# Attention and feed-forward layer on one core: the two lengths of score bursts trade units, and blocks of other matmuls go ahead of the fourth score

## The reference

```python
Q, K, V = x @ Wq.T + bq, x @ Wk.T + bk, x @ Wv.T + bv     # x: 2 x 1024 x 512; 32 query, 8 key heads of 16
Q, K = rope(Q), rope(K)                                    # one key head serves 4 query heads
w = softmax(Q K^T / 4)
x = layernorm(x + (w V) @ Wo.T + bo)
g, u = x @ gate_w.T * gate_s, x @ up_w.T * up_s            # 1408 inner columns
x = layernorm(x + (silu(g) * u) @ down_w.T * down_s)
```

## Time and profile before

| what | value |
|---|---|
| median of 3 runs | 1063.87 us (1063.75 to 1064.66) |
| the profiled execution | 1064.13 us, span 1062.3 us |
| PE busy | 1026.5 us, 97% |
| DVE busy | 809.5 us, 76% |
| ACT busy | 665.1 us, 63% |
| POOL busy | 266.2 us, 25% |
| weighings u = 0 to 255 in the trace | from 66.83 us to 796.57 us |
| TensorE clock granted | 0.998 of full speed |

### The profile page before, as it was taken

One profiled execution on the slowest core, in us unless ns is written; L12 is line 12 of the kernel. 1 busy time (PEld: TensorE's weight loads), 2 busy tenths in 40 slices (PEclk: granted clock), 3 DMA queues, 4 the chain that ended last, 5 costly groups with the idle time before them and its releaser, 6 DMA issues.

```text
span 1062.3 us, 15699 instructions
## 1 busy us (share of the span) xinstructions
PE 1026.5 (97%) x5858; PEld 536.8 (51%) x5858; DVE 809.5 (76%) x1199; ACT 665.1 (63%) x1346; POOL 266.2 (25%) x227
## 2 busy tenths in 40 slices
PE   8999999999999999999999999999999999999996
PEld 3643344433443433443444443333337888888885
DVE  4899978899779799779988899999803475662535
ACT  2368877788778788778766678888863431222221
POOL 2751030141335422246200042844100000000002
PEclk9999999999999999999999999999999999999999
DMA  5274417243142512344140446531217510402011
GB/s 200 80 196 126 106 35 213 52 97 78 52 115 75 105 56 54 82 108 105 34 78 12 116 120 150 124 121 37 93 68 193 166 40 9 111 28 52 1 39 42
DMA packets 64432, 94.87 MB, mean 89 GB/s; under 512 B 37536, under 2 KB 37920, under 8 KB 62272
## 3 DMA queue, kind: packets, MB, share of 16 engines
q1 hardware_dynamic: 63776, 93.10, 33.2%
q10 hardware_dynamic: 576, 0.72, 0.2%
HBM read 53.95 MB, written 27.00 MB: 76 GB/s over the span
## 4 chain that ended last, share of the span: by engine, by line
PE 80%; DVE 10%; ACT 6%; issue 2%; DMA 1%; SPq 0%; POOL 0%; DVEq 0%; POOLq 0%
PE PS L448 21%; PE PV L467 20%; PE PSA L537 15%; PE PS L554 5%; PE PSA L426 5%; DVE nmx L964 5%; PE PS L365 4%; ACT Bn L756 3%; PE PS L493 2%; PE PSA L493 2%; DVE nmx L960 2%; DVE nmx L957 2%; ACT Bn L765 2%; PE PV L554 2%; PE PSA L365 1%
## 5 line engine op out<-in xcount | busy, mean ns | idle before, releaser
L756 ACT ACTIVATE Bn<-PS 128x512 f32<-128x512 f32 x1146 | 548.8, 559 | 125.0 <-PE PS L448 111.1
L448 PE MATMUL PS<-Qt,Kt 50*128 50x512 f32 x1146 | 391.7, 434 | 20.0 <-ACT Bn L756 18.7
L426 PE MATMUL PSA<-Kt,Qt 48*128 48x512 f32 x1024 | 390.0, 459 | 2.2 <-DVE Kt L936 0.8
L964 DVE TENSOR_REDUCE nmx<-PSA 128x1 f32<-128x1024 f32 x256 | 312.2, 1219 | 61.0 <-PE PSA L426 59.8
L448 PEld LDWEIGHTS PS<-Qt,Kt 50*128 50x128 f32 x1146 | 184.4, 184 | 323.6 <-ACT Bn L756 312.7
L467 PE MATMUL PV<-Bn 128*32 128x512 f32 x2048 | 272.8, 605 | 0.0
L426 PEld LDWEIGHTS PSA<-Kt,Qt 48*128 48x128 f32 x1024 | 174.6, 183 | 21.7 <-DVE nmx L964 6.2
L960 DVE TENSOR_REDUCE nmx<-PSA 128x1 f32<-128x512 f32 x256 | 174.5, 682 | 1.4 <-PE PSA L426 1.1
L957 DVE TENSOR_REDUCE nmx<-PSA 128x1 f32<-128x512 f32 x256 | 174.3, 681 | 0.0
L537 PE MATMUL PSA<-x1Th,wr 128*128 128x512 f32 x344 | 135.0, 393 | 0.8 <-DVE sg L1052 0.5
L537 PE MATMUL PSA<-x1Tl,wr 128*128 128x512 f32 x344 | 134.7, 392 | 0.0
(11 more groups left out here) (166 smaller groups left out, 919.4 us busy)
## 6 DMA issues: line engine op xcount, KB each, us to landing
Qt<-pscr SPq DMA_DIRECT2D x90, 128.0 KB, 4.9
A<-in_wf SPq DMA_DIRECT2D x11, 768.0 KB, 6.3
wr<-A SPq DMA_DIRECT2D x33, 256.0 KB, 2.9
pscr<-A SPq DMA_DIRECT2D x16, 512.0 KB, 3.7
vscr<-Bn SPq DMA_DIRECT2D x32, 256.0 KB, 2.0
Kt<-pscr SPq DMA_DIRECT2D x90, 64.0 KB, 2.3
A<-A SPq DMA_DIRECT2D x16, 256.0 KB, 3.7
Bn<-vscr SPq DMA_DIRECT2D x8, 512.0 KB
```

Source lines behind the costliest of these rows:

```text
L426: op = e.matmul(PSA[:, 2 * s + h, :], Qt[n % 3][p:p + NC_, g % 2, 128 * qt:128 * qt + 128], Kt[n % 3][p:p + NC_, 512 * h:512 * h + 512], s ...
L448: e.matmul(PS2[:, i, cols], Kt[n % 3][rows, 128 * kt:128 * kt + 128], Qt[n % 3][rows, g % 2, 512 * qh + cols.start:512 * qh + cols.stop], ...
L756: e.activation(Pb[c % NP_][:, cols], PS2[:, score_bank[c, p], cols], ACT.Exp, scale=0.25).then_inc(*act_exp.next(piece(c, p)))
L964: e.tensor_reduce(nmx[:, hh % 2, c0:c0 + 1], slot_pair(s), AX.XY, ALU.max, negate=True).then_inc(*dve_max[s].next(k))
```

## The change

The bursts trade places. `weigh(u - 1)` now stands behind the third score of odd units and behind the fourth of even ones, and the cut score is the fourth of odd units (`c % 8 == 7`). The block of an odd unit goes directly behind that weighing, ahead of the unit's fourth score (`background`), and uses the banks that are free there (`free_banks`). ACT moves a projection out ahead of the fourth exponential. DVE takes only the first half of the unit's second step ahead of its work for the block, and the second half, with the closing of the round, behind it. The closing is cut into three functions with the same four operations.

PE at the first block of the loop, before: the last matmul of the block, then a whole burst of three with its weighing, then the cut score.

```diff
--- before.py
+++ after.py
@@ -291,7 +291,7 @@
 
         def pieces(c):
 
-            return [slice(0, 128), slice(128, 512)] if c % 8 == 3 and c < 4 * SPLIT else [slice(0, 512)]
+            return [slice(0, 128), slice(128, 512)] if c % 8 == 7 and c < 4 * SPLIT else [slice(0, 512)]
 
         score_bank = {}
         for c in range(4 * U):
@@ -302,7 +302,7 @@
             return c if p == len(pieces(c)) - 1 else (c, p)
 
         def free_banks(u):
-            last = score_bank[4 * u + 3, len(pieces(4 * u + 3)) - 1]
+            last = score_bank[4 * u + 2, 0]
             return (last + 1) % 3, last
 
         def ffn_slots(x):
@@ -663,6 +663,20 @@
                     project_half(1, 0, 0, (1, 2, 3))
                 else:
                     project_half(1, 1, 3, ((0, 1), (2, 3))[k - 2])
+            def background(u):
+                at_u, pair = divmod(u, 16), free_banks(u)
+                if at_u in project_at:
+                    for h, i in enumerate(pair):
+                        project_half(project_at[at_u], h, i, (0, 1, 2, 3))
+                if at_u == values_at:
+                    for t in range(8):
+                        value_rows(1, t, pair[t // 4])
+                if at_u in out_at:
+                    t2 = out_at[at_u]
+                    out_project(False, 0, t2, [bank(i) for i in pair], [bank_free[i] for i in pair])
+                    for j, i in enumerate(pair):
+                        bank_free[i] = dve_y.at((False, 0, 2 * t2 + j))
+
             for u in range(SPLIT):
                 at_u = divmod(u, 16)
                 for g in range(4):
@@ -670,19 +684,9 @@
                     advance(1)
                     if len(pieces(4 * u + g)) == 2:
                         scores(u, g, 1)
-                    if u >= 1 and g == (2, 3)[u % 2]:
+                    if u >= 1 and g == (3, 2)[u % 2]:
                         weigh(u - 1)
-                if at_u in project_at:
-                    for h, i in enumerate(free_banks(u)):
-                        project_half(project_at[at_u], h, i, (0, 1, 2, 3))
-                if at_u == values_at:
-                    for t in range(8):
-                        value_rows(1, t, free_banks(u)[t // 4])
-                if at_u in out_at:
-                    t2, pair = out_at[at_u], free_banks(u)
-                    out_project(False, 0, t2, [bank(i) for i in pair], [bank_free[i] for i in pair])
-                    for j, i in enumerate(pair):
-                        bank_free[i] = dve_y.at((False, 0, 2 * t2 + j))
+                        background(u)
                 if at_u == (15, 1):
                     flag_sum()
                 if at_u == (15, 2):
@@ -892,11 +896,11 @@
                 at_u = divmod(u, 16)
                 for g in range(4):
                     exponent(u, g)
+                    if g == 2 and at_u in project_at:
+                        for h, i in enumerate(free_banks(u)):
+                            evacuate_raw(project_at[at_u], h, i)
                 if u >= 1:
                     finish(u - 1)
-                if at_u in project_at:
-                    for h, i in enumerate(free_banks(u)):
-                        evacuate_raw(project_at[at_u], h, i)
                 if at_u in rope_end and rope_end[at_u][1] in ("h0", "h1"):
                     round_half(rope_end[at_u][0], int(rope_end[at_u][1] == "h1"))
                 if at_u == (15, 2):
@@ -944,7 +948,7 @@
                     bv[:, :].rearrange("p (o v c) -> p o v c", o=1, v=NKV).to_broadcast([128, 4, NKV, HD]),
                     ALU.add).then_inc(*dve_val.next((b, h)))
 
-            def maximum(k):
+            def maximum(k, halves=(0, 1)):
                 if k >= len(stream):
                     return
                 s, hh = slot_of(k), k // 16
@@ -953,24 +957,28 @@
                 if hh >= 2:
                     w.wait_ge(*dve_ms.at(("low", hh - 2)))
                 if by_halves(k):
-                    w.wait_ge(*pe_max.at((k, 0)))
-                    e.tensor_reduce(nmx[:, hh % 2, 16 + c0:17 + c0], slot_pair(s)[:, 0, :], AX.X, ALU.max, negate=True).then_inc(
-                        *dve_max[s].next((k, 0)))
-                    w.wait_ge(*pe_max.at(k))
-                    e.tensor_reduce(nmx[:, hh % 2, c0:c0 + 1], slot_pair(s)[:, 1, :], AX.X, ALU.max, negate=True).then_inc(
-                        *dve_max[s].next(k))
+                    for h in halves:
+                        w.wait_ge(*pe_max.at((k, 0) if h == 0 else k))
+                        col = nmx[:, hh % 2, c0 + 16 * (h == 0):c0 + 16 * (h == 0) + 1]
+                        e.tensor_reduce(col, slot_pair(s)[:, h, :], AX.X, ALU.max, negate=True).then_inc(
+                            *dve_max[s].next((k, 0) if h == 0 else k))
                 else:
                     w.wait_ge(*pe_max.at(k))
                     e.tensor_reduce(nmx[:, hh % 2, c0:c0 + 1], slot_pair(s), AX.XY, ALU.max, negate=True).then_inc(
                         *dve_max[s].next(k))
-                if k % 16 == 15:
+                if 1 in halves and k % 16 == 15:
+                    join_max(hh)
+                    split_max(hh)
                     turn_max(hh)
 
-            def turn_max(hh):
+            def join_max(hh):
                 top, rest = nmx[:, hh % 2, 0:16], nmx[:, hh % 2, 16:24]
                 for k in (16 * hh + 14, 16 * hh + 15):
                     w.wait_ge(*dve_max[slot_of(k)].at(k))
                 e.tensor_tensor(top[:, 0:8], top[:, 0:8], rest, ALU.min).then_inc(*dve_ms.next(("join", hh)))
+
+            def split_max(hh):
+                top = nmx[:, hh % 2, 0:16]
                 w.wait_ge(*dve_ms.at(("join", hh)))
                 if hh >= 1:
                     w.wait_ge(*dve_ms.at(("turn", hh - 1)))
@@ -978,6 +986,8 @@
                 w.wait_ge(*dve_ms.at(("high", hh)))
                 e.tensor_tensor(msp[:, 16:32], top, msp[:, 0:16].bitcast(F32), ALU.subtract).then_inc(
                     *dve_ms.next(("low", hh)))
+
+            def turn_max(hh):
                 w.wait_ge(*dve_ms.at(("low", hh)))
                 if hh >= 2:
                     w.wait_ge(*max_out[hh % 2].at(hh - 2))
@@ -1216,14 +1226,19 @@
             for u in range(SPLIT):
                 at_u = divmod(u, 16)
                 maximum(next(steps))
-                maximum(next(steps))
-                if at_u in norm_at:
-                    first_norm(False, 0, norm_at[at_u])
-                if at_u == values_at:
-                    for h, i in enumerate(free_banks(u)):
-                        add_values(1, h, i)
-                if at_u in out_at:
-                    add_rows(False, 0, out_at[at_u], [bank(i) for i in free_banks(u)])
+                k = next(steps)
+                if at_u in norm_at or at_u in out_at or at_u == values_at:
+                    maximum(k, (0,))
+                    if at_u in norm_at:
+                        first_norm(False, 0, norm_at[at_u])
+                    if at_u == values_at:
+                        for h, i in enumerate(free_banks(u)):
+                            add_values(1, h, i)
+                    if at_u in out_at:
+                        add_rows(False, 0, out_at[at_u], [bank(i) for i in free_banks(u)])
+                    maximum(k, (1,))
+                else:
+                    maximum(k)
                 if at_u in recip_at:
                     reciprocal(recip_at[at_u])
                 if at_u == (15, 0):
```

## The result

| kernel | median, us | lowest to highest, us |
|---|---|---|
| before | 1063.91 (12 runs) | 1063.25 to 1064.90 |
| after | 1065.94 (12 runs) | 1062.42 to 1068.38 |

The ratio is 1.0021, 95% interval 1.0014 to 1.0029: the change makes the kernel 0.2% slower. The forecast was 1057.3, its range ended at 1062.5, and "faster" had 0.78. It was wrong. The profiled execution of the changed kernel took 1068.05 us, so 2.1 over its median. Note the spread: the runs of before lie within 1.65 us of each other, those of after within 6, and the granted clock of a run of after lies between 0.989 and 0.997.

A forecast was written before the change was run, and what follows sets the result against it. A loop of engines close to balance, bursts of five at ACT's pace, of three at PE's; −15.0 + 3.5 + 2.3 + 0.8 + 1.0 = −7.4, plus 0.6 for thin cover, gives 1057.3 from 1064.13; range 1053.5 to 1062.5 us.

The forecast's parts named there:

- The beat: Loop's undisturbed distance between weighings: 3.03 us for a burst of five, 1.89 for three; claimed to stay 4.92 per pair.
- The 30 copies: ACT's copies of PV, moved behind the fourth exponential of even units: 0 instead of 0.50 each, minus 15.0 us.
- the thin cover: Room before a PV copy delays the loop: 0.18 on PE's side, 0.08 on ACT's; 0.02 per copy added, 0.6 us.
- The closings: DVE's closings of rounds, moved behind a burst of five: 19 at 0.50 against 14 costing 6.0 us, plus 3.5.
- Reciprocals and halves at blocks: DVE's work after blocks: five reciprocals at 0.46, 2.3 us, and five late halves at 0.17, 0.8; plus 3.1 us.
- Roundings: ACT's roundings cost 0.53 in a burst of five, nothing in ACT's gap: nine pay against seven, plus 1.0 us.
- The block costs the same: Projection block at its new place behind the weighing: 6.18 us again, so 0 for the move.
- Start, end, POOL and SP, 0 ± 1 us: Loop's first and last weighings cancel within 0.5 us; POOL and SP wait for the same counts, maxima at most one block later.
- Start and end: First weighing one score earlier, loop's last one burst earlier, cancelling within 0.5 us; the 266 us behind the loop untouched.
- the held weighing: Rival: PE, released by the copy's end, starts the next weighing 0.30 late; 30 copies cost 9.0, about 1066; chance 0.04.

The follow-up runs named there:

- the bursts alone: The kernel before with only the bursts of three and five traded, the blocks staying at the end of their units: 1053.25 us, 0.9899 of before.

## Why the prediction was wrong

- *The beat, right.* 1.89 and 3.04 in every kernel of the study.
- *The 30 copies, right.* −14.8 for −15.0; the thin cover (0.6 us set aside) wasn't used up, and the doubled copy, at 0.50 each, shows where it ends.
- *The closings, right.* 19 in the open, 16 of them at 0.50 to 0.53 for a forecast 0.50, two at 0.40 and 0.46, and that of u = 107, whose excess is counted below.
- *Reciprocals and halves at blocks, right.* Five units with a reciprocal at 0.39 to 0.64, two of these with a late half in it, and three more late halves at 0.16: 3.0 in all for 3.1. (The 0.64 behind u = 131, a projection without a late half, is 0.18 over its forecast and unexplained.)
- *Roundings, right.* Nine at 0.52; moved to even units they cost nothing, in two kernels.
- *The block costs the same, right within 0.3 us,* though against the bursts alone its new place costs 2.1 over the eleven: left at the end of the unit a block would have been cheaper than before, which I didn't look for.
- *"Start, end, POOL and SP, 0 ± 1 us": the step that failed.* It said that POOL and SP wait for the same counts and that the closed maxima "come at most one block later than now". Both hold: the code of POOL and SP is unchanged, and at the first block the write of the maxima goes out 6.4 us later (142.75 for 136.37). What it left out is the next instruction in SP's queue. There the swap stands behind the write of the maxima and behind a second transfer that waits for the first, so a closing moved behind the block moves the swap by 4.5 us, and POOL's rope with it. I had counted when the maxima are needed, not who stands behind them. Its price in the profiled execution was 9.5 us: 1.9 at three roundings that wait for POOL, 2.1 at the closing that POOL held, and 5.5 in the low clock afterwards. Putting the swap ahead took 6.8 us back by the medians and 8.5 by the extras. The 0.5 at u = 207 is another term that was put at nothing: there the second transfer of the maxima came later behind the first, which the queue's order doesn't explain.
- *Start and end, within the ±1 us:* the first weighing comes 0.25 earlier (66.58 for 66.83), one burst of five more instead of one of three up to weighing 243 costs 1.2, and behind that the profiles agree within 0.2.
- *The rivals.* The time of the held weighing (1066) was met, but not by its mechanism: the load was held by the copy, and no weighing came late. None of the five named POOL or the clock. The 0.78 for faster was thus lost to one thing, and that is no mis-sized term but a queue not followed.

Two things stay open. The granted clock fell behind idle stretches of PE of 1.15, 1.94 and 0.97 us at u = 89, 107 and 145, but not behind the 1.22 us at u = 33 and not behind the 0.7 us where POOL was set beside the closings; what decides it, the runs don't show. And the spread of the changed kernel's runs (6 us) goes roughly with its clock (1062.42 at 0.997, 1068.14 at 0.989, though 1068.38 at 0.994), which suggests that these falls come in some executions and not in others; only the profiled one has a trace.

## What to carry to other kernels

When a step moves later on one engine, write down what stands behind each of its waiters in every in-order queue, the DMA-issuing one above all, and follow those to the next engine; here 4.5 us in a queue that is hardly busy cost some 7 of the 10.7 us that the bursts had brought. On a balanced pipeline price a change by what stands beyond the undisturbed beat, place by place: each term that the forecast had held to 0.3 us. Try the two halves of a change apart before keeping both: one was worth −10.7 us and the other +12.7, and the first, with the roundings moved to the other parity, made −16 to −17.
